# FFN by half tiles: two W1 chunks for 256 tokens to a unit, and the last tile's first two blocks normed at mid-tile

## Chip, cores and metric

The kernel runs on one core of one Trainium2 chip. The metric is device time in microseconds (us) of one execution; the median of several runs counts. TensorE is called PE, VectorE DVE, ScalarE ACT, GpSimd POOL; SP is the queue that issues the transfers.

## The reference

8192 tokens of 512 features pass through two blocks, each with a layer norm ahead and one behind, and a residual. The second block is the one that the change touches; its weights are made ternary (-1, 0, 1).

```python
def _layernorm(x, eps=1e-05):
    m = jnp.mean(x, axis=-1, keepdims=True); v = jnp.var(x, axis=-1, keepdims=True)
    return (x - m) / jnp.sqrt(v + eps)

# attention-like block: projection, gate, depthwise convolution of 3, scan, output projection, norm
uv = x @ in_proj_w + in_proj_b                 # u, v: 512 each
v_local = dwconv(silu(v)); h = a * h + ssm_b * v_local; y = ssm_c * h + ssm_d * v_local
out = layernorm((u * silu(y)) @ out_proj_w + out_proj_b + x) * ln_w + ln_b
# FFN block
h = gelu(x @ ternary(W1).T + b1)               # W1: 2048 x 512
out = h @ ternary(W2).T + b2                   # W2: 512 x 2048
# both
x = x + _layernorm(attn(_layernorm(x)))
x = x + _layernorm(ffn(_layernorm(x)))
```

## The kernel before

The tokens are taken in 16 tiles (NT) of 512 (TT). A tile is four blocks (NB) of 128 tokens, one token to a partition. Matmul operands are split into a high and a low half in f16, so that two or three f16 matmuls stand for one in f32; the ternary weights are exact in fp8 and need no split.

**Steps.** Every engine runs its own hand-written order, and semaphores join them. From step s = 3 on a loop over `LATER` does the same on all engines: step s works on the FFN of tile fa = s - 2, on the gate, output projection and norms of tile c = s - 1, on the first norm and the v projection of tile n = s + 1, and on the final norm and store of tile e = s - 3 (`tiles`, line 257). On ACT and DVE each piece of work carries a number (the `AT_...` constants, lines 54 to 70), and `run` (line 81) issues the pieces in the order of these numbers; the FFN's unit j has numbers near j, so 13.3 means "after unit 13's gelu". PE's order is written out in lines 733 to 769.

**The FFN** (fa) of a tile goes in 16 units (FC = 2048/128), one for each chunk of 128 rows of W1:

- `f1(t, j)` (line 537, PE): 8 matmuls of 512 columns into one of two PSUM banks `f1b`: for each of 4 k, the W1 chunk as weights and the high, then the low half of the transposed tile `x3T` as moving data. Its first unit waits for the transposes of all four blocks (`wait_tile`, line 290), every unit for the gelu of two units before, which frees the bank.
- `gelu(t, j)` (line 1603, ACT): PSUM to `gg`, bias from the chunk's b1. `hi(t, j)` (line 1613, ACT) rounds it to f16, `lo(t, j)` (line 801, DVE) makes the rest.
- `f2(t, j)` (line 567, PE): for each of the four blocks q, two matmuls with a 128 x 128 part of h as weights and the W2 chunk (512 columns) as moving data, added up in four banks `f2b[q]`. It follows f1 by a lag of 4 units (`LAG`), in the last tile by 5 (`LAG_END`). Its first unit waits until the four `f_add` of the tile before have read the banks.

In steps before the last two, f1 of units 0 to 8 comes first, with f2 of 0 to 4 in it (five f1 stand in a row at the start), then u, the rest of these f2, o, half of v, and then f1 of units 9 to 15 (again several in a row) with the other f2 and the rest of v.

**The final norm** of a tile is done one step later: `f_add` (line 811, DVE) reads `f2b[j]`, scales it and adds b2 into `hb`; `f_stats` and `aggr` make mean and variance, POOL's `rstd_f` (line 2063) the factors, ACT's `ffn_norm` (line 1628) applies them, POOL's `finish` (line 2081) adds the residual, SP stores. f_add(0) waits for the last unit of f2 of its tile, and with it all four.

**The last tile** ends block by block: `f2_last` (line 556) does the last five units for block 0, then for block 1, 2 and 3, each block signalled by `f2_sum`. Behind all units DVE runs lines 1589 to 1598: for each block `last_block` (f_add, stats, aggregate), and `last_sum` with the residual; block 3 goes through `last_centre` and `last_out`. `less_shift` (line 979), which subtracts a part of block-wise means from the residual, comes at 13.3 for all four blocks. ACT norms blocks 0 to 2 behind its last unit (lines 2019 to 2021), POOL makes the factors of each block (`rstd_last`, line 2071).

**SP** (lines 455 to 469) issues in each step the four stores of tile e, the load of a later tile, and the transposes t1 and t3. The transposes of `x3T` for the next tile wait for f1's last unit of the present one.

Of the kernel before, what the change touches and what calls it, by code (L numbers as in the profile page):

```python
# [24 lines left out]
P = 128  # L25
D = 512
TT = 512
NB = TT // P
KC = D // P
LAG = 4  # L30
X_SLOTS = 4
G_SLOTS = 5
H_SLOTS = 6
T_SLOTS = 4
EPS = 1e-5
ACT_SCALE = 2048.0
# [7 lines left out]
ACT = mybir.ActivationFunctionType  # L44
# [3 lines left out]
BIN, CW, CB, LA, SB, SC, SD, B1 = 0, 8, 20, 24, 28, 32, 36, 40  # L48
# [15 lines left out]
AT_SILU_LAST, AT_GATE_LAST, AT_GATE_HI_LAST = 16.15, (15.0, 15.1), 16.5  # L64
AT_LO_LAST = (7.65, 8.95, 9.6, 10.6, 11.65, 12.2, 12.9)
AT_T3_HI_PAIR = (16.2, 16.4, 16.6, 16.8)
AT_XC = 13.3
AT_LO_PAIR = (0.45, 1.3, 1.9, 2.4, 3.4, 4.6, 6.0, 7.3)
LAG_END = 5
AT_V = (8.9, 8.95, 16.3, 17.2)  # L70


W1_CHUNK, W2_CHUNK = "w1", "w2"
# [7 lines left out]
def run(items):  # L81

    for _, work in sorted(items, key=lambda item: item[0]):
        work()


def spread(at, step, works):

    return [(at + step * i, w) for i, w in enumerate(works)]


def build(nc, x, w_in, w_out, w1t, w2t, params, rows, out):
# [21 lines left out]
    place = {chunk: o for o, chunk in enumerate(ORDER)}  # L114

    with ExitStack() as ctx:
# [11 lines left out]
        w1 = sb("w1", [P, KC, FF], F8)  # L128
# [153 lines left out]
        def wait_transposed(eng, m):  # L282

            kind, t, j = blocks[m]
            if (kind, t) == ("t3", 0):
                eng.wait_ge(x3_mm, halves_x3.index((1, j)) + 1)
            else:
                eng.wait_ge(transposed[m % T_SLOTS], 16 * by_dma[m])

        def wait_tile(eng, kind, t):  # L290

            for j in range(NB - T_SLOTS, NB):
                wait_transposed(eng, block_no[kind, t, j])

        def bank(kind, t, i):
            if (kind, t) == ("v", 0):
# [25 lines left out]
        def x3T_of(t):  # L322

            return x1T[:, t % 2] if t == NT - 2 else x3T
# [148 lines left out]
        def _(pe):  # L473
# [63 lines left out]
            def f1(t, j):  # L537
                i = FC * t + j
                if t == 0:
                    pe.wait_ge(w_ok, last_of(W1_CHUNK, range(KC * (j // BQ), KC * (j // BQ) + KC)))  # L540
                if i < 2:
                    pe.wait_ge(h_ok, i + 1)
                if j == 0 and t > 0:
                    wait_tile(pe, "t3", t)
                elif j == 0:
                    pe.wait_ge(x3_cp, len(halves_x3))
                if i >= 2:
                    pe.wait_ge(gelu_ok, i - 1)
                b, src = f1b[i % 2], x3T_of(t)
                for k in range(KC):  # L550
                    w = w1[:, k, j * P:(j + 1) * P]
                    pe.matmul(b[:, :], w, src[:, k, :], start=k == 0, stop=False)  # L552
                    mm = pe.matmul(b[:, :], w, src[:, KC + k, :], start=False, stop=k == KC - 1)  # L553
                mm.then_inc(f1_mm, 1)

            def f2_last():

                for q in range(NB):
                    for j in range(FC - LAG_END, FC):
                        if q == 0:  # L560
                            pe.wait_ge(hl_ok, FC * (NT - 1) + j + 1)
                        i, qs = FC * (NT - 1) + j, slice(q * P, (q + 1) * P)
                        pe.matmul(f2b[q][:, :], h_hi[:, i % H_SLOTS, qs], w2[:, j, :], start=False, stop=False)
                        mm = pe.matmul(f2b[q][:, :], h_lo[:, i % H_SLOTS, qs], w2[:, j, :], start=False, stop=j == FC - 1)
                    mm.then_inc(f2_sum, 1)

            def f2(t, j):
                i = FC * t + j
                if j == 0 and t > 0:
                    pe.wait_ge(f_ok, NB * t)  # L570
                elif j == 0:
                    pe.wait_ge(h_ok, NB)
                    pe.wait_ge(v_ok, 3 * KC)
                    pe.wait_ge(thr_ok, 4)
                    pe.wait_ge(u_cp, 2)
                pe.wait_ge(hl_ok, i + 1)
                if t == 0:
                    pe.wait_ge(w_ok, place[W2_CHUNK, j] + 1)
                for q in range(NB):
                    qs = slice(q * P, (q + 1) * P)  # L580
                    pe.matmul(f2b[q][:, :], h_hi[:, i % H_SLOTS, qs], w2[:, j, :], start=j == 0, stop=False)  # L581
                    mm = pe.matmul(f2b[q][:, :], h_lo[:, i % H_SLOTS, qs], w2[:, j, :], start=False, stop=j == FC - 1)  # L582
                mm.then_inc(f2_mm, 1)
# [189 lines left out]
        def _(ve_):  # L773
# [35 lines left out]
                                         op0=ALU.mult, op1=ALU.subtract).then_inc(hl_ok, 1)  # L809

            def f_add(e, j):
                if e == NT - 1:
                    ve_.wait_ge(f2_sum, j + 1)
                elif j == 0:
                    ve_.wait_ge(f2_mm, FC * (e + 1))
                if e + 1 < NT - 1:
                    ve_.wait_ge(x3_lo, NB * (e + 1) + j + 1)
                else:
                    ve_.wait_ge(out_st[j], 16 * e)
                ve_.scalar_tensor_tensor(out=hb[:, j, :], in0=f2b[j][:, :], scalar=f_inv[:, 0:1], in1=b2_row,  # L820
                                         op0=ALU.mult, op1=ALU.add).then_inc(f_ok, 1)
# [157 lines left out]
            def less_shift(j):  # L979

                t = NT - 1
                xsj = xs[:, t % X_SLOTS, j, :]
                ve_.wait_ge(rs_ok[2], NT)
                ve_.tensor_scalar(xsj, xsj, c0[:, t % 4, j:j + 1], None, ALU.subtract).then_inc(xc_ok, 1)

            def last_block(j):

                f_add(NT - 1, j)
                f_stats(NT - 1, j)
                aggr(4, NT - 1, j)  # L990
# [5 lines left out]

            def last_out(j):

                ve_.wait_ge(cen_ok, 1)
                ve_.wait_ge(rs_ok[4], NT + j)  # L1000
                ve_.scalar_tensor_tensor(out=hb[:, j, :], in0=hb[:, j, :], scalar=rs4[:, j:j + 1],
                                         in1=xs[:, (NT - 1) % X_SLOTS, j, :], op0=ALU.mult, op1=ALU.add).then_inc(fin_last, 1)

            def last_sum(j):

                ve_.wait_ge(fn_ok, NB * (NT - 1) + j + 1)
                ve_.tensor_tensor(hb[:, j, :], hb[:, j, :], xs[:, (NT - 1) % X_SLOTS, j, :], ALU.add).then_inc(fin_last, 1)

# [494 lines left out]
            for s in LATER:  # L1503
# [4 lines left out]
                if s == NT:  # L1508
                    items += norms(c) + [(at, lambda j=j: t_lo("t3", c, j)) for j, at in enumerate(AT_T3_LO_LAST)]
                if s == NT + 1:  # L1510
                    items += spread(AT_XC, .01, [lambda j=j: less_shift(j) for j in range(NB)])
                if c is not None and s < NT:
                    items += conv_scan(c)
                if fa is not None:
# [52 lines left out]
                if s == NT - 1:  # L1567
# [18 lines left out]
                        aggr(4, NT - 3, j)  # L1586
                    for j in range(NB):
                        aggr(1, NT - 1, j)
            ve_.wait_ge(xc_ok, NB)
            last_block(0)  # L1590
            last_block(1)
            last_sum(0)
            last_block(2)
            last_sum(1)
            last_block(3)
            last_centre(3)
            last_sum(2)
# [4 lines left out]
        def _(act):  # L1602
            def gelu(t, j):
                i = FC * t + j
                act.wait_ge(f1_mm, i + 1)
                if i < G_SLOTS:
                    act.wait_ge(w_ok, place[W1_CHUNK, i] + 1)
                if i >= G_SLOTS:
                    act.wait_ge(hl_ok, i - G_SLOTS + 1)
                act.activation(gg[:, i % G_SLOTS, :], f1b[i % 2][:, :], ACT.Gelu,  # L1610
                               bias=par[:, B1 + j:B1 + j + 1], scale=1.0 / ACT_SCALE).then_inc(gelu_ok, 1)

# [359 lines left out]
            for s in LATER:  # L1972
# [7 lines left out]
                    items += ffn(fa, range(half(s)))  # L1980
                if s == NT:
                    items += [(at, lambda j=j: t_hi("t3", c, j)) for j, at in enumerate(AT_T3_HI_LAST)]
                run(items)
                if s >= NT:
                    continue
# [30 lines left out]
                if s == NT - 1:  # L2016
                    for b in range(2, KC):
                        gate_hi(NT - 1, b)
            for j in range(NB - 1):
                act.wait_ge(rs_ok[4], NT + j)  # L2020
                ffn_norm(NT - 1, j)


        @block.gpsimd
# [245 lines left out]
```

## Time and profile before

| | |
|---|---|
| runs | 1421.04, 1421.73, 1422.21 us; median 1421.73 |
| span of the profiled execution, first to last instruction | 1420.3 us |
| its own device time | not listed; the runs lie 0.7 to 1.9 us above the span |
| PE busy | 1400.8 us, 6506 matmuls and as many weight loads |
| DVE, ACT, POOL busy | 1116.8, 878.2, 422.3 us |
| mean granted clock of TensorE | 0.999 |

Read it thus: the span is what the profile explains, the median what is measured. A PE record of a 512-column matmul lasts 379 ns, but the next one begins after about 216, since matmuls are pipelined and their ends are modelled. So time on PE is told from starts, not from the sum of the records.

### The profile page before, as it was taken

Reading aid. Unit: us, or ns where it says so; the run is one execution under the profiler, and the core shown is the slowest. Engines: PE = TensorE matmul, PEld = TensorE weight load, DVE = VectorE, ACT = ScalarE, POOL = GpSimd, SP = SyncE. Lnnn points to the kernel's source line nnn. Section 1 sums busy time; section 2 is a strip of 40 time slices with the busy share of each in tenths; the row PEclk is TensorE's granted clock in tenths of the full one; section 3 lists DMA queues with packets and bytes.
Section 4 is the critical chain, followed back from the end, with each engine's and each line's share of the span. In section 5 each row is a group of like instructions: output and inputs, shape, how many; then the busy total and the mean of one; then the engine's idle time right before and its main releaser. Section 6 shows DMA issues by size and latency. Waiting matters only on the chain.

```text
span 1420.3 us, 18989 instructions
## 1 busy us (share of the span) xinstructions
PE 1400.8 (99%) x6506; PEld 640.0 (45%) x6506; DVE 1116.8 (79%) x1889; ACT 878.2 (62%) x1264; POOL 422.3 (30%) x522
## 2 busy tenths in 40 slices
PE   7999999999999999999999999999999999999997
PEld 4444444444444444444444444444444444444443
DVE  7999987868779686796867878677796877998744
ACT  7999665656556565675656756565565656753443
POOL 5234241322314232042331413223142321523221
PEclk9999999999999999999999999999999999999999
DMA  8703221211311122121311203113111221001200
GB/s 245 254 36 90 60 83 20 78 30 38 82 30 60 30 61 59 30 66 25 89 30 31 82 16 82 31 38 82 31 60 30 53 67 30 30 1 30 60 31 30
DMA packets 155984, 82.00 MB, mean 58 GB/s; under 512 B 132720, under 2 KB 132720, under 8 KB 155760
## 3 DMA queue, kind: packets, MB, share of 16 engines
q1 hardware_dynamic: 155888, 80.79, 22.0%
q8 instruction: 51, 0.84, 0.2%
q14 instruction: 45, 0.37, 0.1%
HBM read 31.49 MB, written 16.78 MB: 34 GB/s over the span
## 4 chain that ended last, share of the span: by engine, by line
PE 85%; DVE 4%; issue 3%; POOL 1%; ACT 0%; POOLq 0%; DVEq 0%; ACTq 0%
PE f2b L581 14%; PE f2b L582 14%; PE f1b L552 14%; PE f1b L553 14%; PE misc L520 6%; PE misc L519 6%; PE misc L518 6%; PE misc L533 3%; PE misc L534 3%; PE misc L532 3%; DVE bn L789 1%; DVE vl L865 0%; DVE vl L874 0%; DVE ring L807 0%; POOL rsc L2038 0%
## 5 line engine op out<-in xcount | busy, mean ns | idle before, releaser
L581 PE MATMUL f2b<-w,ring 128*128 128x512 fp8e5 x1004 | 380.5, 379 | 1.2 <-DVE ring L807 0.9
L582 PE MATMUL f2b<-w,ring 128*128 128x512 fp8e5 x1004 | 380.5, 379 | 0.0
L552 PE MATMUL f1b<-x3T,w 128*128 128x512 f16 x960 | 363.8, 379 | 0.1
L553 PE MATMUL f1b<-x3T,w 128*128 128x512 f16 x960 | 363.8, 379 | 0.0
L1610 ACT ACTIVATE ring<-f1b,par 128x512 f32<-128x512 f32 x256 | 175.2, 684 | 227.8 <-PE f1b L553 227.5
L2037 POOL TENSOR_SCALAR ve<-mv 128x4 f32<-128x4 f32 (+2 forms) x89 | 35.4, 398 | 725.5 <-DVE mv L799 725.4
L807 DVE SCALAR_TENSOR_TENSOR ring<-ring,f_sc 128x512 f16<-128x512 f32 x256 | 212.5, 844 | 37.6 <-ACT ring L1620 37.4
L1620 ACT ACTIVATE ring<-ring,f_sc 128x512 f16<-128x512 f32 x256 | 180.1, 710 | 0.0
L518 PE MATMUL misc<-x1T,win_hi 128*128 128x512 f16 x456 | 172.8, 379 | 0.0
L520 PE MATMUL misc<-x1T,win_lo 128*128 128x512 f16 x456 | 172.8, 379 | 0.0
L519 PE MATMUL misc<-x1T,win_hi 128*128 128x512 f16 x456 | 172.8, 379 | 0.0
L581 PEld LDWEIGHTS f2b<-w,ring 128*128 128x128 f16 x1004 | 98.2, 98 | 121.1 <-DVE ring L807 2.4
L582 PEld LDWEIGHTS f2b<-w,ring 128*128 128x128 f16 x1004 | 98.2, 98 | 118.0
L552 PEld LDWEIGHTS f1b<-x3T,w 128*128 128x128 fp8e5 x960 | 93.9, 98 | 114.4 <-issue 1.5
L553 PEld LDWEIGHTS f1b<-x3T,w 128*128 128x128 fp8e5 x960 | 93.9, 98 | 112.7
L1729 ACT ACTIVATE vb<-misc,par,inv_sig 128x512 f32<-128x512 f32 x54 | 41.9, 776 | 140.3 <-PE misc L520 140.1
L789 DVE BATCH_NORM_STATS2 bn<-hb 128x6 f32<-128x512 f32 x184 | 118.8, 679 | 0.2
L865 DVE SCALAR_TENSOR_TENSOR vl<-vb,par,vl 128x512 f32<-128x512 f32 x128 | 105.9, 866 | 0.9 <-POOL vb L2142 0.8
L2093 POOL TENSOR_TENSOR hb<-hb,row 128x512 f32<-128x512 f32 x56 | 80.7, 1444 | 85.7 <-ACT hb L1661 85.7
L2083 POOL TENSOR_TENSOR hb<-hb,xs 128x512 f32<-128x512 f32 x60 | 99.6, 1687 | 18.6 <-ACT hb L1631 18.6
L532 PE MATMUL misc<-wo_hi,g_hi 128*128 128x512 f16 x240 | 91.0, 379 | 0.4 <-DVE g_lo L909 0.3
L533 PE MATMUL misc<-wo_lo,g_hi 128*128 128x512 f16 x240 | 91.0, 379 | 0.0
(227 smaller groups left out, 2015.3 us busy)
## 6 DMA issues: line engine op xcount, KB each, us to landing
out_dram<-hb SPq DMA_DIRECT2D x64, 256.0 KB, 2.0
xs<-x_dram SPq DMA_DIRECT2D x14, 1024.0 KB, 5.4
ring<-w1t_dram SPq DMA_DIRECT2D x3, 1024.0 KB, 13.2
stage<-w2t_dram SPq DMA_DIRECT2D x3, 1024.0 KB, 8.0
x1T<-tp SPq DMA_TRANSPOSE x68, 3.1
xs<-x_dram SPq DMA_DIRECT2D x4, 256.0 KB, 3.4
stage<-w_in_dram SPq DMA_DIRECT2D x4, 256.0 KB, 5.7
xs<-x_dram SPq DMA_DIRECT2D x2, 512.0 KB, 7.2
```

Of the source, the lines that this page charges most:

```text
L518: pe.matmul(o[:, :], wh, x1T[:, s_, k, :], start=k == 0, stop=False)
L519: pe.matmul(o[:, :], wh, x1T[:, s_, KC + k, :], start=False, stop=False)
L520: mm = pe.matmul(o[:, :], wl, x1T[:, s_, k, :], start=False, stop=k == KC - 1)
L532: pe.matmul(out_[:, :], g_hi[:, k, js], wo_hi[:, k, :], start=c > 0 and k == 0, stop=False)
L533: pe.matmul(out_[:, :], g_hi[:, k, js], wo_lo[:, k, :], start=False, stop=False)
L552: pe.matmul(b[:, :], w, src[:, k, :], start=k == 0, stop=False)
L553: mm = pe.matmul(b[:, :], w, src[:, KC + k, :], start=False, stop=k == KC - 1)
L581: pe.matmul(f2b[q][:, :], h_hi[:, i % H_SLOTS, qs], w2[:, j, :], start=j == 0, stop=False)
L582: mm = pe.matmul(f2b[q][:, :], h_lo[:, i % H_SLOTS, qs], w2[:, j, :], start=False, stop=j == FC - 1)
L807: ve_.scalar_tensor_tensor(out=h_lo[:, i % H_SLOTS, :], in0=gg[:, i % G_SLOTS, :], scalar=f_sc[:, 0:1], in1=h_hi[:, i % H_SLOTS, :], op0=A ...
L1610: act.activation(gg[:, i % G_SLOTS, :], f1b[i % 2][:, :], ACT.Gelu, bias=par[:, B1 + j:B1 + j + 1], scale=1.0 / ACT_SCALE).then_inc(gelu_o ...
L1620: act.activation(h_hi[:, i % H_SLOTS, :], gg[:, i % G_SLOTS, :], ACT.Copy, scale=f_sc[:, 0:1]).then_inc(hh_ok, 1)
```

## The change

From tile 1 on, a unit is no longer one W1 chunk for 512 tokens, but the two chunks p and p + 8 for one half (256 tokens) of the tile: units 0 to 7 do blocks 0 and 1, units 8 to 15 blocks 2 and 3. Tile 0 stays as it was.

- f1: 16 matmuls of 256 columns where 8 of 512 were; a bank holds the two chunks side by side. Unit 0 waits for the transposes of blocks 0 and 1 alone, unit 8 for those of blocks 2 and 3.
- gelu: two activations of 256 columns, each with its chunk's bias. hi and lo stay one instruction of 512 each.
- f2: 8 matmuls of 512 columns as before, now 2 blocks x 2 chunks x 2 halves. Unit 0 waits for f_add of the blocks 0 and 1 of the tile before, unit 8 for those of 2 and 3.
- f_add(0) waits for unit 7 of its tile, f_add(2) for unit 15.
- Last tile: f2_last handles blocks 2 and 3 only, with 20 matmuls each (it was four blocks of 10). DVE's last_block(0) and (1) move to 10.3 and 12.3, last_sum(0) and (1) to 14.25 and 15.22, less_shift to 9.45, 10.45, 11.45, 12.45; ACT's norms of blocks 0 and 1 to 13.3 and 14.3. Behind the units stay blocks 2 and 3.

```diff
-AT_XC = 13.3
+AT_XC = 9.45
+AT_FIRST_LAST = (10.3, 12.3)
+AT_FIRST_LAST_NORM, AT_FIRST_LAST_OUT = (13.3, 14.3), (14.25, 15.22)
...
+    PAIRS = FC // 2
+
+    def unit(j):
+
+        h, p = divmod(j, PAIRS)
+        return h, (p, p + PAIRS)
+
+    def half_done(t, h):
+
+        return FC * t + (PAIRS if t > 0 and h == 0 else FC)
...
-                if j == 0 and t > 0:
-                    wait_tile(pe, "t3", t)
+                if j % PAIRS == 0 and t > 0:
+                    wait_blocks(pe, "t3", t, range(2 * (j // PAIRS), 2 * (j // PAIRS) + 2))
...
+                if t > 0:
+                    h, chunks = unit(j)
+                    for n, chunk in enumerate(chunks):
+                        for k in range(KC):
+                            w, o_ = w1[:, k, chunk * P:(chunk + 1) * P], b[:, n * TH:(n + 1) * TH]
+                            pe.matmul(o_, w, src[:, k, h * TH:(h + 1) * TH], start=k == 0, stop=False)
+                            mm = pe.matmul(o_, w, src[:, KC + k, h * TH:(h + 1) * TH], start=False, stop=k == KC - 1)
+                    mm.then_inc(f1_mm, 1)
+                    return
...
-                for q in range(NB):
+                for q in (2, 3):
                     for j in range(FC - LAG_END, FC):
-                        if q == 0:
+                        if q == 2:
                             pe.wait_ge(hl_ok, FC * (NT - 1) + j + 1)
...
+            def f2_block(t, j, q):
+
+                i, (h, chunks) = FC * t + j, unit(j)
+                for n, chunk in enumerate(chunks):
+                    qs = slice(n * TH + (q - 2 * h) * P, n * TH + (q - 2 * h + 1) * P)
+                    pe.matmul(f2b[q][:, :], h_hi[:, i % H_SLOTS, qs], w2[:, chunk, :],
+                              start=chunk == 0, stop=False)
+                    mm = pe.matmul(f2b[q][:, :], h_lo[:, i % H_SLOTS, qs], w2[:, chunk, :],
+                                   start=False, stop=chunk == FC - 1)
+                return mm
...
-                if j == 0 and t > 0:
-                    pe.wait_ge(f_ok, NB * t)
+                if j % PAIRS == 0 and t > 0:
+                    pe.wait_ge(f_ok, NB * (t - 1) + 2 + 2 * (j // PAIRS))
...
-                if e == NT - 1:
-                    ve_.wait_ge(f2_sum, j + 1)
-                elif j == 0:
-                    ve_.wait_ge(f2_mm, FC * (e + 1))
+                if e == NT - 1 and j >= 2:
+                    ve_.wait_ge(f2_sum, j - 1)
+                elif j % 2 == 0:
+                    ve_.wait_ge(f2_mm, half_done(e, j // 2))
...
-                    items += spread(AT_XC, .01, [lambda j=j: less_shift(j) for j in range(NB)])
+                    items += spread(AT_XC, 1, [lambda j=j: less_shift(j) for j in range(NB)])
+                    items += [(at, lambda j=j: last_block(j)) for j, at in enumerate(AT_FIRST_LAST)]
+                    items += [(at, lambda j=j: last_sum(j)) for j, at in enumerate(AT_FIRST_LAST_OUT)]
...
-            ve_.wait_ge(xc_ok, NB)
-            last_block(0)
-            last_block(1)
-            last_sum(0)
             last_block(2)
-            last_sum(1)
             last_block(3)
             last_centre(3)
             last_sum(2)
...
+                if t > 0:
+                    for n, chunk in enumerate(unit(j)[1]):
+                        ts = slice(n * TH, (n + 1) * TH)
+                        ins = act.activation(gg[:, i % G_SLOTS, ts], f1b[i % 2][:, ts], ACT.Gelu,
+                                             bias=par[:, B1 + chunk:B1 + chunk + 1], scale=1.0 / ACT_SCALE)
+                    ins.then_inc(gelu_ok, 1)
+                    return
...
+                if s == NT + 1:
+                    items += [(at, lambda j=j: last_norm(j)) for j, at in enumerate(AT_FIRST_LAST_NORM)]
...
-            for j in range(NB - 1):
-                act.wait_ge(rs_ok[4], NT + j)
-                ffn_norm(NT - 1, j)
+            last_norm(2)
```

## Rows read from the trace of the kernel before

**Rows 1.** The page: busy time by engine, and the chain that ended last.

```profile
PE 1400.8 (99%) x6506; PEld 640.0 (45%) x6506; DVE 1116.8 (79%) x1889; ACT 878.2 (62%) x1264; POOL 422.3 (30%) x522
...
PE f2b L581 14%; PE f2b L582 14%; PE f1b L552 14%; PE f1b L553 14%; PE misc L520 6%; PE misc L519 6%; PE misc L518 6%; PE misc L533 3%; PE misc L534 3%; PE misc L532 3%; DVE bn L789 1%; DVE vl L865 0%; DVE vl L874 0%; DVE ring L807 0%; POOL
```

**Rows 2.** Waits of PE: us in total, times, longest.

```profile
PE f1b L588 <- ACT tp L1704: 7.9, 1, 7.9
...
PE f2b L581 <- DVE ring L807: 0.9, 2, 0.8
```

**Rows 3.** Timeline of PE (start, us), first matmuls of two tiles' f1.

```profile
253.06 0.38 PE L552 MATMUL f1b<-x3T,w 128*128 128x512 f16 x1
...
771.05 0.38 PE L552 MATMUL f1b<-x3T,w 128*128 128x512 f16 x1
```

**Rows 4.** Groups of instructions, f1's first matmuls on PE: busy us, mean ns | idle.

```profile
L552 PE MATMUL f1b<-x3T,w 128*128 128x512 f16 x960 | 363.8, 379 | 0.1
```

**Rows 5.** 128-column matmuls: timeline of PE, and durations (min/median/max) of two lines.

```profile
81.88 0.61 PE L615 MATMUL f1b<-ident_h,tp 128*128 128x128 f16 x8
...
L615 PE MATMUL f1b<-ident_h,tp x16: 219/219/230, 81.9 to 85.6; 128*128 128x128 f16 x16
...
51.69 0.83 PE L605 MATMUL f1b<-ones 128*128 128x128 f32 x6
...
L605 PE MATMUL f1b<-ones x6: 273/275/275, 51.7 to 52.2; 128*128 128x128 f32 x6
```

**Rows 6.** Timeline of PE at two tile boundaries, last of f2 and first of f1.

```profile
857.17 0.38 PE L582 MATMUL f2b<-w,ring 128*128 128x512 fp8e5 x1
857.53 0.38 PE L552 MATMUL f1b<-x3T,w 128*128 128x512 f16 x1
...
1029.98 0.38 PE L582 MATMUL f2b<-w,ring 128*128 128x512 fp8e5 x1
...
1030.45 0.38 PE L552 MATMUL f1b<-x3T,w 128*128 128x512 f16 x1
```

**Rows 7.** ACT: Sign of 512 and of 2048 columns (groups), gelu and hi in the timeline.

```profile
L1758 ACT ACTIVATE w<-ring,thr 128x512 fp8e5<-128x512 f32 x4 | 2.9, 728 | 0.0
...
L1746 ACT ACTIVATE w<-ring,thr 128x2048 fp8e5<-128x2048 f32 x2 | 3.9, 1994 | 0.2 <-DVE thr L1186 0.2
...
515.71 0.69 ACT L1610 ACTIVATE ring<-f1b,par 128x512 f32<-128x512 f32 x1 [1.04 <-PE f1b L553]
516.29 0.71 ACT L1620 ACTIVATE ring<-ring,f_sc 128x512 f16<-128x512 f32 x1
```

**Rows 8.** Timelines of ACT and PE: gelu of unit 9, first matmul of f1(11).

```profile
571.33 0.69 ACT L1610 ACTIVATE ring<-f1b,par 128x512 f32<-128x512 f32 x1
...
572.49 0.38 PE L552 MATMUL f1b<-x3T,w 128*128 128x512 f16 x1
```

**Rows 9.** Timeline of DVE: the four f_add at a boundary.

```profile
512.26 2.73 DVE L820 SCALAR_TENSOR_TENSOR hb<-f2b,f_inv,row 128x512 f32<-128x512 f32 x4 [3.99 <-PE f2b L582]
```

**Rows 10.** Timeline in the last steps: PE behind DVE's lo, DVE behind POOL.

```profile
1273.77 2.08 DVE L963 SCALAR_TENSOR_TENSOR xs<-hb,rsc,xs 128x512 f32<-128x512 f32 x3 [1.52 <-POOL c L2061]
...
1276.57 0.39 PE L581 MATMUL f2b<-w,ring 128*128 128x512 fp8e5 x1 [0.77 <-DVE ring L807]
...
1331.54 0.39 PE L581 MATMUL f2b<-w,ring 128*128 128x512 fp8e5 x1 [0.17 <-DVE ring L807]
```

**Rows 11.** Timelines of PE and DVE at the end: last matmul, f_add(1), last_sum(1), f_add(3).

```profile
1412.49 0.38 PE L564 MATMUL f2b<-w,ring 128*128 128x512 fp8e5 x1
...
1408.59 0.75 DVE L820 SCALAR_TENSOR_TENSOR hb<-f2b,f_inv,row 128x512 f32<-128x512 f32 x1 [0.41 <-PE f2b L564]
...
1412.99 0.66 DVE L1007 TENSOR_TENSOR hb<-hb,xs 128x512 f32<-128x512 f32 x1
1413.57 0.75 DVE L820 SCALAR_TENSOR_TENSOR hb<-f2b,f_inv,row 128x512 f32<-128x512 f32 x1
```

**Rows 12.** Timeline of DVE in the last tile: lo(10).

```profile
1390.06 0.75 DVE L807 SCALAR_TENSOR_TENSOR ring<-ring,f_sc 128x512 f16<-128x512 f32 x1 [2.70 <-ACT ring L1620]
```

More of the change, by code:

```diff
@@ L66 @@
 AT_T3_HI_PAIR = (16.2, 16.4, 16.6, 16.8)
-AT_XC = 13.3
+AT_XC = 9.45
+AT_FIRST_LAST = (10.3, 12.3)
+AT_FIRST_LAST_NORM, AT_FIRST_LAST_OUT = (13.3, 14.3), (14.25, 15.22)
 AT_LO_PAIR = (0.45, 1.3, 1.9, 2.4, 3.4, 4.6, 6.0, 7.3)
 LAG_END = 5
+TH = TT // 2
 AT_V = (8.9, 8.95, 16.3, 17.2)
@@ L288, in wait_transposed, with wait_blocks @@
                 eng.wait_ge(transposed[m % T_SLOTS], 16 * by_dma[m])
+        def wait_blocks(eng, kind, t, js):
+            for j in js:
+                wait_transposed(eng, block_no[kind, t, j])
         def wait_tile(eng, kind, t):
-            for j in range(NB - T_SLOTS, NB):
-                wait_transposed(eng, block_no[kind, t, j])
+            wait_blocks(eng, kind, t, range(NB))
         def bank(kind, t, i):
@@ L556, in f2_last @@
             def f2_last():
-                for q in range(NB):
+                for q in (2, 3):
                     for j in range(FC - LAG_END, FC):
-                        if q == 0:
+                        if q == 2:
                             pe.wait_ge(hl_ok, FC * (NT - 1) + j + 1)
-                        i, qs = FC * (NT - 1) + j, slice(q * P, (q + 1) * P)
-                        pe.matmul(f2b[q][:, :], h_hi[:, i % H_SLOTS, qs], w2[:, j, :], start=False, stop=False)
-                        mm = pe.matmul(f2b[q][:, :], h_lo[:, i % H_SLOTS, qs], w2[:, j, :], start=False, stop=j == FC - 1)
+                        mm = f2_block(NT - 1, j, q)
                     mm.then_inc(f2_sum, 1)
+            def f2_block(t, j, q):
[7 more added lines that the diff above has]
+                return mm
             def f2(t, j):
                 i = FC * t + j
-                if j == 0 and t > 0:
-                    pe.wait_ge(f_ok, NB * t)
+                if j % PAIRS == 0 and t > 0:
+                    pe.wait_ge(f_ok, NB * (t - 1) + 2 + 2 * (j // PAIRS))
                 elif j == 0:
@@ L576, in f2 @@
                 pe.wait_ge(hl_ok, i + 1)
-                if t == 0:
-                    pe.wait_ge(w_ok, place[W2_CHUNK, j] + 1)
+                if t > 0:
+                    for q in range(2 * (j // PAIRS), 2 * (j // PAIRS) + 2):
+                        mm = f2_block(t, j, q)
+                    mm.then_inc(f2_mm, 1)
+                    return
+                pe.wait_ge(w_ok, place[W2_CHUNK, j] + 1)
                 for q in range(NB):
@@ L997, in last_out @@
             def last_out(j):
+                ve_.wait_ge(xc_ok, j + 1)
                 ve_.wait_ge(cen_ok, 1)
@@ L1004, in last_sum @@
             def last_sum(j):
+                ve_.wait_ge(xc_ok, j + 1)
                 ve_.wait_ge(fn_ok, NB * (NT - 1) + j + 1)
@@ L1609, in gelu @@
                     act.wait_ge(hl_ok, i - G_SLOTS + 1)
+                if t > 0:
+                    for n, chunk in enumerate(unit(j)[1]):
[3 more added lines that the diff above has]
+                    ins.then_inc(gelu_ok, 1)
+                    return
                 act.activation(gg[:, i % G_SLOTS, :], f1b[i % 2][:, :], ACT.Gelu,
@@ L1632, in ffn_norm, with last_norm @@
                                scale=rs4[:, j:j + 1]).then_inc(fn_ok, 1)
+            def last_norm(j):
+                act.wait_ge(rs_ok[4], NT + j)
+                ffn_norm(NT - 1, j)
             def centre_tap(c, b):
```

## The prediction

> **What bounds the kernel now.** I read the page first. TensorE (PE) is busy for 1400.8 of the 1420.3 us of the span, and the chain that ended last lies nearly all on it, in the matmuls of the projections and of the two FFN products [rows 1]. So I asked what PE waits for. The list of its waits holds 7.9 us once at the start, and behind that little: the one that concerns the FFN is 0.9 us in two waits [rows 2]. A change can win only four things: columns through PE, time per column, the rare waits, and the stretch after the last matmul. It can lose by making a matmul dearer, or by making PE wait for ScalarE (ACT), VectorE (DVE) or a transfer. A busy share of 99% doesn't say how dense the matmuls are, because a record of 379 ns covers its successor. The starts say it: from the first matmul of tile 2's f1 (253.06) to that of tile 8's (771.05) lie six steady tiles of 400 matmuls (128 each for f1 and f2, 48 each for u, v and o), so 517.99/2400 = 215.8 ns from start to start [rows 3].
>
> **f1 in halves.** In tiles 1 to 15 a unit of f1 issued 8 matmuls of 512 columns and now issues 16 of 256. That is 15 x 16 x 8 = 1920 matmuls (line 552 has 64 records for each of the 15 tiles whose f1 reads x3T, 960 [rows 4], and line 553 as many), which become 3840 with the same columns in all. The price is what a matmul costs beyond its columns. No row has 256 columns. The nearest are the 128-column f16 matmuls of the x3 transposes: eight span 0.61 us, the last of them 0.219 long, so (0.61 - 0.219)/7 = 55.9 ns from start to start [rows 5]. Between 128 and 512 columns that makes (215.8 - 55.9)/384 = 0.4165 ns a column, which is 2.4 GHz, and leaves 55.9 - 53.3 = 2.5 ns that each matmul pays whatever its length. Twice 256 columns is then about 218.4 ns instead of 215.8: 2.6 ns x 1920 = **+5.0 us**, all on PE. Weight loads double too. Every matmul has a load of its own (6506 of each [rows 1]), and the transposes keep 55.9 ns with theirs, so matmuls 109 ns apart hide them. From below the price is 0 (two halves cost a whole). From above I take the f32 matmuls on 128 columns: six span 0.83 us, the last 0.275, so 111 ns apart [rows 5], and 2 x 111 - 215.8 = 6.2 ns or 11.9 us. I take 5.0, because the transposes have the same type of moving data.
>
> The Trainium skill has a rule against this change: "Each matmul has ~60 cycle overhead on TRN2" (TensorEngine Tiling (Array Packing), Instruction Overhead). By it the 1920 added matmuls would cost 25 ns each, an estimate of 48 us. Starts 55.9 ns apart [rows 5] leave no room for such a surcharge on 53.3 ns of columns, so at this length the trace disagrees.
>
> **f2 and the waits of PE.** A unit of f2 issued 8 matmuls for four blocks and now issues 8 for two: same number, same 512 columns, no cost. f1(t,0) waits for two transposed blocks instead of four, f2(t,0) for two added blocks of the tile before. The rest of each wait moves to unit 8, some 20 us on, when all has long been there. In two of the boundaries before f1(t,0) the step between starts was 0.36 and 0.47 us instead of 0.216 [rows 6], 0.14 and 0.26 us lost where f1's waits stand; at the others it was the usual step. I count both as gone: **-0.4 us** (bound: 0, if it wasn't the later blocks).
>
> **Gelu in halves.** Two activations of 256 columns, each with its own bias, replace one of 512 in 240 units. No row has a 256-column gelu. Sign takes 728 ns for 512 columns and 1994 for 2048, so 0.82 ns a column, and a gelu of 0.69 us frees ACT after 0.58 (515.71 to 516.29) [rows 7]. Halved: 0.58 - 0.21 = 0.37 to the second start, plus 0.69 - 0.21 = 0.48, so 0.85 instead of 0.69: **0.16 us later** per unit, and 39 us more of ACT, which is busy 878 of 1420 [rows 1]. Bounds: 0, and 0.58 if a half costs what a whole does. What hides it: where f1 units follow each other without f2, the bank of f1(j) comes free with gelu(j-2). The tightest is f1(11) at 572.49, with gelu(9) over at 571.33 + 0.69 = 572.02, so 0.47 us [rows 8]; 0.16 fits, 0.58 doesn't. Behind gelu(9) on ACT stand gelu(10) and hi(9); a unit then needs 0.74 + 0.6 us of ACT in the 1.75 us that f1 takes, so nothing piles up. At a tile's start two d_conv stand between gelu(3) and gelu(4), but f1(6), which needs gelu(4), comes after two f2 units. Cost: 0.
>
> **DVE.** At each boundary DVE has been idle 4 us when it takes the four f_add in one go of 2.73 us [rows 9]. Blocks 0 and 1 are complete at mid-tile now, so two f_add move into that idle time, and the DVE work behind them, lo(0) to lo(4) with it, comes up to 1.3 us earlier (the scans at most as early as d_conv, which ACT brings 0.16 later). POOL's rstd_f and finish and SP's stores follow the same work and come no later. None of it is on the path: 0.
>
> **The pair of last tiles.** PE is idle 0.77 us before 1276.57 and 0.17 before 1331.54, for DVE's lo [rows 10]; with the 0.16 by which a record outlasts the step between starts, 0.93 and 0.33 us lost. DVE itself had stood in its norms behind POOL (1.52 us before 1273.77) [rows 10]. That chain starts with o, so f1 units that PE does meanwhile don't delay it: 6 in the first case and some 11 in the second, each 8 x 2.6 ns = 0.02 us longer, come out of the waits. **-0.35 us**, bounds 0 and -1.3 (both gone).
>
> **The end.** The last matmul starts at 1412.49 and is over at 1412.87, but f_add(3) starts at 1413.57, behind last_sum(1), which began at 1412.99 [rows 11]. f_add(1) wasn't so blocked: it started at 1408.59, and its block was complete 20 matmuls before block 3, at 1412.87 - 4.32 = 1408.55 [rows 11]. Now blocks 0 and 1 are normed before, and block 2 is complete 4.3 us ahead of block 3, while its f_add, stats and aggregate take some 1.7. So f_add(3) can start at 1412.91: **-0.65 us** (bounds 0 and -1.4, if POOL's chain behind it also runs undisturbed). Behind it stays what was: stats, aggregate, POOL's power, last_out, and the store whose landing ends the kernel. At mid-tile last_block(0) waits on DVE for f2(7), over at about 1393.9, with lo(10) behind it. lo(10) ran at 1390.06 [rows 12] and f2(10) starts 47 matmuls before the last one, at 1402.35; now lo(10) ends at about 1396.7, still 5.6 us ahead. last_norm(0) waits on ACT for POOL until some 1397.3, with gelu(14) behind it, which f1(14) doesn't release before 1399. Cost: 0; were this cover gone, PE would wait about 1 us once.
>
> **Sum.** +5.0 - 0.4 - 0.35 - 0.65 = +3.6 us, give or take 0.7 from the small terms. The span goes from 1420.3 to 1423.9. What lies around it isn't listed for the profiled execution; the median of the runs is 1.43 us above its span, and I keep that: 1421.73 + 3.6 = **1425.3**.
>
> **Rivals.** (A) Half-length matmuls pay 2.5 ns each: 1425.3, chance 0.64. (B) The other side, not slower: the fixed share vanishes at 256 columns. For it: nothing shows that length. Against: it is there at 128 and at 512. Price 0, so -1.4 in all, 1420.3; it decides once the added matmul costs under 0.7 ns (0.12). (C) They behave as the f32 ones, 111 ns apart, because loads or their dispatch bind in runs of 80; for it, the longest run of short f16 ones in the trace is twelve. +11.9 - 1.4, so 1432.2 (0.08). (D) ACT becomes the releaser: half a gelu costs nearly the whole 0.58, f1(11) waits 0.11 us in each of 13 tiles, and the five f1 in a row at a tile's start run at ACT's pace (1.16 + 0.6 against 1.75), some hundredths each: about +2, 1427.3; against it, the slope of [rows 7] (0.08). (E) The early blocks don't do what they are there for, and block 3 still finds DVE busy: the 0.65 stays, 1425.9 (0.07). (F) Tens of ns on each added matmul: 25 x 1920 = 48 us, 1470 (0.01).
>
> **Numbers.** 0.2%, 2.84 us, is about what a measurement of this kernel can tell from no change, so slower means over 1424.6. A lies 0.7 above that, and a quarter of it falls below (the -1.3 bound, a longer gain at the end); with B that makes 0.28 for no change. A gain of 2.84 us needs B, both waits gone and a shorter chain on POOL: 0.03. Slower 0.69. The range takes in A, D, E and part of the way to B and C: 1422.2 to 1429.0.
>
> **What would show it.** On PE 3840 records of 256 columns, starts about 109.2 ns apart, and a steady tile of 86.66 us instead of 86.33. Pairs still 215.8 apart mean B, 222 mean C. No new wait of PE for gelu (line 1610's); one of 0.1 us in each tile means D. A 256-column gelu near 0.48 us. f_add of block 2, not of block 0, first after each boundary. At the end f_add(3) within 0.1 us of the last matmul's end. The forecast is wrong if the steady tile keeps its 86.33 us, or if a wait recurs in every tile.

## The result and the profile after

Changed kernel: median 1425.1 us of 7 runs (1424.7 to 1427.88), before 1421.73 us; the ratio is 1.0029 with a 95% interval of 1.0018 to 1.004. A second set on another occasion gave 1425.42 against 1422.01, ratio 1.0021 (1.0012 to 1.003). So the change makes the kernel 3.4 us slower, 0.2 to 0.3%, as forecast (1425.3, range 1422.2 to 1429.0). Both intervals lie above 1.

The profiled execution of the changed kernel spans 1425.9 us and took 1427.88, the highest of its seven, so it isn't read as a whole but piece by piece. From the page (busy us by engine, the groups of f1 and of gelu):

```profile
PE 1403.4 (98%) x8426; PEld 825.4 (58%) x8426; DVE 1119.8 (79%) x1889; ACT 911.8 (64%) x1504; POOL 414.2 (29%) x522
...
L573 PE MATMUL f1b<-x3T,w 128*128 128x256 f16 x1792 | 397.5, 273 | 0.0
...
L1652 ACT ACTIVATE ring<-f1b,par 128x256 f32<-128x256 f32 x480 | 201.2, 471 | 227.0 <-PE f1b L574 226.7
```

PE has 8426 matmuls, 1920 more than in [rows 1]; ACT has 240 instructions and 33.6 us more (39 forecast). The waits of PE (us in total, times, longest):

```profile
PE f1b L628 <- ACT tp L1755: 7.8, 1, 7.8
PE misc L550 <- DVE hb L968: 2.2, 1, 2.2
PE f1b L628 <- DMA x1T<-tp: 2.0, 3, 1.5
...
PE f2b L597 <- DVE ring L847: 0.8, 1, 0.8
```

There is no wait for a gelu. The second line is a single stall in the straight-line start of the kernel, which the change doesn't touch. It is why the first f1 of tile 1 starts at 168.99 instead of 166.73. The second profiled execution of the same kernel had it at 166.43 and a span of 1422.8.

Timeline of PE, first matmul of f1 in tiles 2 and 8, and four of the starts in a row:

```profile
255.64 0.27 PE L573 MATMUL f1b<-x3T,w 128*128 128x256 f16 x1
255.75 0.27 PE L574 MATMUL f1b<-x3T,w 128*128 128x256 f16 x1
255.86 0.27 PE L573 MATMUL f1b<-x3T,w 128*128 128x256 f16 x1
255.97 0.27 PE L574 MATMUL f1b<-x3T,w 128*128 128x256 f16 x1
...
775.56 0.27 PE L573 MATMUL f1b<-x3T,w 128*128 128x256 f16 x1
```

Six steady tiles take 519.92 us instead of 517.99 [rows 3]: 86.65 us a tile instead of 86.33, 0.32 more for 128 more matmuls, which is 2.5 ns each. The starts, taken over the 3469 steps from one 256-column matmul of f1 on x3T straight to the next, are 109.17 ns apart.

Timeline of DVE at the same boundary as in [rows 9], and in the last microseconds, with PE's last matmul and POOL's last two (L2089 raises the variance to a power; the texts below call it POOL's power):

```profile
515.80 1.41 DVE L860 SCALAR_TENSOR_TENSOR hb<-f2b,f_inv,row 128x512 f32<-128x512 f32 x2 [2.81 <-PE f2b L599]
...
1418.86 0.38 PE L599 MATMUL f2b<-w,ring 128*128 128x512 fp8e5 x1
...
1419.27 0.75 DVE L860 SCALAR_TENSOR_TENSOR hb<-f2b,f_inv,row 128x512 f32<-128x512 f32 x1 [2.62 <-PE f2b L599]
...
1421.41 0.68 DVE L1049 TENSOR_TENSOR hb<-hb,xs 128x512 f32<-128x512 f32 x1
1422.64 0.75 DVE L1042 SCALAR_TENSOR_TENSOR hb<-hb,rs,xs 128x512 f32<-128x512 f32 x1 [0.55 <-POOL rs L2089]
...
1421.05 0.51 POOL L2088 TENSOR_SCALAR ve<-mv 128x1 f32<-128x1 f32 x1 [2.86 <-DVE mv L839]
1421.64 0.86 POOL L2089 TENSOR_TENSOR rs<-ve,mhalf 128x1 f32<-128x1 f32 x1
```

DVE takes two f_add at the boundary, not four. At the end it is idle for 2.6 us before f_add(3), which starts 0.03 us after the last matmul is over (1418.86 + 0.38) instead of 0.70 [rows 11].

The kernel before and both profiled executions of the changed one, cut at the first f1 of a tile (us; the last column runs to the last instruction):

| | tile 1 to 13 | 13 to 14 | 14 to 15 | 15 to last matmul's end | behind it |
|---|---|---|---|---|---|
| before | 1036.39 | 98.74 | 55.60 | 55.42 | 7.46 |
| change | 1039.84 | 99.10 | 55.57 | 55.74 | 6.68 |
| change, second execution | 1039.84 | 99.11 | 55.57 | 55.74 | 6.13 |
| difference, first execution | +3.45 | +0.36 | -0.03 | +0.32 | -0.78 |

The differences of the first execution add up to +3.32 us, against 3.4 in the medians. The last column counts from the modelled end of the last matmul, as the texts below do; from its start it would be 0.38 more (7.83 and 7.05, the numbers in one of the expectations).

### The profile page after: what moved, and what is told of

The parts are those of the page before. It is cut to its first block, busy times and chain, and to the rows that moved or that the text cites. A ratio compares the mean times of both kernels' runs of the same rounds, so it can differ in the third digit from the quotient of the medians.

```text
span 1425.9 us, 23101 instructions
## 1 busy us (share of the span) xinstructions
PE 1403.4 (98%) x8426; PEld 825.4 (58%) x8426; DVE 1119.8 (79%) x1889; ACT 911.8 (64%) x1504; POOL 414.2 (29%) x522
## 4 chain that ended last, share of the span: by engine, by line
PE 86%; DVE 4%; issue 2%; DMA 0%; ACT 0%; POOL 0%; POOLq 0%; DVEq 0%; ACTq 0%
PE f1b L573 14%; PE f1b L574 14%; PE f2b L597 14%; PE f2b L599 14%; PE misc L538 6%; PE misc L536 6%; PE misc L537 6%; PE misc L550 3%; PE misc L552 3%; PE misc L551 3%; PE f2b L622 1%; PE f2b L621 1%; DVE w L1234 0%; DVE g_lo L949 0%; DMA xs<-x_dram 0%
## 5 line engine op out<-in xcount | busy, mean ns | idle before, releaser
L573 PE MATMUL f1b<-x3T,w 128*128 128x256 f16 x1792 | 397.5, 273 | 0.0
L574 PE MATMUL f1b<-x3T,w 128*128 128x256 f16 x1792 | 397.5, 273 | 0.0
L597 PE MATMUL f2b<-w,ring 128*128 128x512 fp8e5 x960 | 363.9, 379 | 0.8 <-DVE ring L847 0.8
L599 PE MATMUL f2b<-w,ring 128*128 128x512 fp8e5 x960 | 363.8, 379 | 0.0
L1652 ACT ACTIVATE ring<-f1b,par 128x256 f32<-128x256 f32 x480 | 201.2, 471 | 227.0 <-PE f1b L574 226.7
L847 DVE SCALAR_TENSOR_TENSOR ring<-ring,f_sc 128x512 f16<-128x512 f32 x256 | 200.4, 796 | 30.1 <-ACT ring L1666 30.0
L574 PEld LDWEIGHTS f1b<-x3T,w 128*128 128x128 fp8e5 x1792 | 175.4, 98 | 32.6
L573 PEld LDWEIGHTS f1b<-x3T,w 128*128 128x128 fp8e5 x1792 | 175.3, 98 | 32.5
L597 PEld LDWEIGHTS f2b<-w,ring 128*128 128x128 f16 x960 | 93.9, 98 | 101.4 <-DVE ring L847 1.8
L599 PEld LDWEIGHTS f2b<-w,ring 128*128 128x128 f16 x960 | 93.9, 98 | 99.5
L905 DVE SCALAR_TENSOR_TENSOR vl<-vb,par,vl 128x512 f32<-128x512 f32 x128 | 119.2, 970 | 0.9 <-POOL vb L2193 0.8
## 6 DMA issues: line engine op xcount, KB each, us to landing
ring<-w1t_dram SPq DMA_DIRECT2D x3, 1024.0 KB, 13.5
```

Source lines behind the costliest of these rows:

```text
L573: pe.matmul(o_, w, src[:, k, h * TH:(h + 1) * TH], start=k == 0, stop=False)
L574: mm = pe.matmul(o_, w, src[:, KC + k, h * TH:(h + 1) * TH], start=False, stop=k == KC - 1)
L597: pe.matmul(f2b[q][:, :], h_hi[:, i % H_SLOTS, qs], w2[:, chunk, :], start=chunk == 0, stop=False)
L847: ve_.scalar_tensor_tensor(out=h_lo[:, i % H_SLOTS, :], in0=gg[:, i % G_SLOTS, :], scalar=f_sc[:, 0:1], in1=h_hi[:, i % H_SLOTS, :], op0=A ...
L1652: ins = act.activation(gg[:, i % G_SLOTS, ts], f1b[i % 2][:, ts], ACT.Gelu, bias=par[:, B1 + chunk:B1 + chunk + 1], scale=1.0 / ACT_SCALE)
```

## Experiments

The kernel before was run again beside the experiments: its median was 1422.76 us (26 runs) beside e1, e2, e3 and e6, and 1422.01 us (31 runs) beside e4, e5, e7 and a2. Each ratio below is against these.

### f1 alone in halves (e1_f1_256)

```diff
+                if t > 0:
+                    for n in range(TT // 256):
+                        cs = slice(n * 256, (n + 1) * 256)
+                        for k in range(KC):
+                            w = w1[:, k, j * P:(j + 1) * P]
+                            pe.matmul(b[:, cs], w, src[:, k, cs], start=k == 0, stop=False)
+                            mm = pe.matmul(b[:, cs], w, src[:, KC + k, cs], start=False, stop=k == KC - 1)
+                    mm.then_inc(f1_mm, 1)
+                    return
```

> The kernel before with nothing but f1's matmuls of tiles 1 to 15 cut into two of 256 columns (same chunk, same unit, same gelu, same waits). Theory (each matmul pays 2.5 ns beyond its columns): starts of f1 109.2 ns apart, steady tile 86.65 us instead of 86.33, in all +4.8 us less about 0.2 that the waits of the last tiles swallow; no gain at the end: 1426.3 if before is at 1421.7. Rival (the steady tile grew because of the half-tile order, the second gelu or the waits at unit 8): starts still 107.9 ns apart, tile 86.33, no change against before.

Measured: 1427.16 us, ratio 1.0033 (1.0023 to 1.0044), 4.4 us slower than before. Steady tile 86.65 us, starts 109.17 ns apart. Between two tiles:

```profile
252.99 0.27 PE L555 MATMUL f1b<-x3T,w 128*128 128x256 f16 x1
253.10 0.27 PE L556 MATMUL f1b<-x3T,w 128*128 128x256 f16 x1
```

The whole growth of the steady tile comes with the cut of the matmuls alone. The end stayed at 7.46 us. From tile 13 to 14 it took 98.94 us, 0.20 more than before: of the 0.32 for its matmuls, 0.12 came out of PE's wait for lo.

### f1 in quarters (e2_f1_128)

The same edit with 128 in place of 256.

> The kernel before with f1's matmuls of tiles 1 to 15 cut into four of 128 columns, runs of up to 160 short matmuls. Theory (2.5 ns a matmul): 128 x 3 x 2.5 = 0.96 us more a tile, 87.29 us, starts 55.9 ns apart, in all +14.4 us. Rival (in long runs weight loads or the supply of instructions bind, as twelve short ones in a row could not show): starts clearly over 56 ns, new idle time of PE's loads put down to issue, more than 1 us a tile; at 81 ns apart it would be 128 x 4 x 25 ns = 12.8 us a tile.

Measured: 1434.74 us (4 runs), ratio 1.0088 (1.0069 to 1.0107), 12.0 us slower. Groups of f1's matmuls and of their weight loads:

```profile
L556 PE MATMUL f1b<-x3T,w 128*128 128x128 f16 x3584 | 412.6, 219 | 0.0
...
L555 PEld LDWEIGHTS f1b<-x3T,w 128*128 128x128 fp8e5 x3584 | 350.6, 98 | 13.9 <-issue 0.4
```

The steady tile took 87.29 us, 0.96 more than before, and the starts were 55.8 ns apart over 7053 steps. The loads waited 0.4 us in all for issue. So runs of 160 short matmuls keep the price of 2.5 ns each; in them neither loads nor the supply of instructions bind. The median is 2.4 us under the 14.4 of the theory. In the profiled execution the stretches from tile 1 to the last matmul grew by 13.5 us (the stalls at boundaries and for lo gave way for the rest), and its end was 0.6 us shorter than in before's, with POOL's power at 0.60 us instead of 1.02; the remaining 0.9 us lies within the spread of the medians.

### Gelu alone in halves (e3_gelu_halves)

```diff
+                if t > 0:
+                    for ts in (slice(0, TT // 2), slice(TT // 2, TT)):
+                        ins = act.activation(gg[:, i % G_SLOTS, ts], f1b[i % 2][:, ts], ACT.Gelu,
+                                             bias=par[:, B1 + j:B1 + j + 1], scale=1.0 / ACT_SCALE)
+                    ins.then_inc(gelu_ok, 1)
+                    return
```

> The kernel before with nothing but the gelu of tiles 1 to 15 cut into two activations of 256 columns. Theory (0.16 us later per unit, hidden behind 0.47 us and more): no change, within 0.5 us; steady tile 86.33 us, gelu records of 471 ns. Rival (ACT's lateness reaches PE): waits of PE for the gelu line in each tile, some tenths of a us each, +2 us or more in all.

Measured: 1422.88 us, ratio 0.9994 (0.9985 to 1.0003): no change, and no wait of PE for gelu. But there is one place where the lateness gets through. Timelines of ACT and DVE in tile 13:

```profile
1258.65 0.84 ACT L1612 ACTIVATE ring<-f1b,par 128x256 f32<-128x256 f32 x2 [0.89 <-PE f1b L553]
1259.38 0.72 ACT L1626 ACTIVATE ring<-ring,f_sc 128x512 f16<-128x512 f32 x1
...
1260.13 0.75 DVE L807 SCALAR_TENSOR_TENSOR ring<-ring,f_sc 128x512 f16<-128x512 f32 x1 [0.28 <-ACT ring L1626]
```

DVE waits 0.28 us for hi(13,9), where it waited 0.15 before, with the norms queued behind it. From there to PE's wait for lo, DVE's work comes 0.15 us late against the tile's start, the step between starts at that wait is 1.30 us instead of 1.15, and tile 13 to 14 took 98.89 us, 0.15 more than before, with not one matmul more. But it comes back: PE arrives late at its next wait for lo too, but that lo comes when it did before (128.4 us after the tile's start in both), the step there is 0.40 us instead of 0.55, and tile 14 to 15 took 55.45 us, 0.15 less. From tile 13 to 15 both kernels take 154.3 us, within 0.01 of each other.

### The last tile alone by half tiles (e6_last_tile_only)

The change with its conditions `t > 0` made `t == NT - 1` in f1, f2, gelu and half_done; tiles 1 to 14 keep the old units and waits.

> Half-tile units in the last tile alone, tiles 1 to 14 as before; last tile's first two blocks normed at mid-tile as in the change. Theory: 128 more matmuls cost 0.3 us, the end after the last matmul shrinks from 7.83 us to 7.05 (0.78), steady tile 86.33: 0.45 us faster than before, about 1421.3, and 3.8 us faster than the change. Rival (the shorter end needs the half tiles throughout, or was chance): the end stays at 7.8 us, 1422.0.

Measured: 1421.81 us, ratio 0.9997 (0.9988 to 1.0007). Steady tile 86.333, last tile 0.32 us longer, 6.67 us behind the last matmul. The end is shorter without half tiles elsewhere, and the loss of the change is gone. Against before it can't be told from no change, so the 0.45 us faster of the theory is neither shown nor excluded.

### Norms of the last tile behind all units (e4_norms_behind)

```diff
-                    items += [(at, lambda j=j: last_block(j)) for j, at in enumerate(AT_FIRST_LAST)]
-                    items += [(at, lambda j=j: last_sum(j)) for j, at in enumerate(AT_FIRST_LAST_OUT)]
...
+            last_block(0)
+            last_block(1)
+            last_sum(0)
             last_block(2)
+            last_sum(1)
             last_block(3)
```

ACT's norms of blocks 0 and 1 stand behind its last unit as well.

> The changed kernel, but the last tile's blocks 0 and 1 are added, normed and summed behind all units, as before, instead of at mid-tile; order of f1 and f2 as in the change. Theory 1 (the end is shorter because block 3 is complete 20 matmuls behind block 2, which leaves DVE time to clear what came earlier): DVE works blocks 0 to 2 off from lo(15) on, some 6 us, and is free when block 3 is complete: f_add(3) still within 0.3 us of the last matmul's end, time as the change within 0.3 us. Rival (the norms at mid-tile are what shortens the end): f_add(3) starts 0.7 us or more behind the last matmul's end, 0.7 us slower than the change.

Measured: 1425.44 us, ratio 1.0026 (1.0017 to 1.0036); the change beside it had 1425.42. Timeline of DVE:

```profile
1412.37 0.74 DVE L860 SCALAR_TENSOR_TENSOR hb<-f2b,f_inv,row 128x512 f32<-128x512 f32 x1
...
1417.33 0.74 DVE L860 SCALAR_TENSOR_TENSOR hb<-f2b,f_inv,row 128x512 f32<-128x512 f32 x1
...
1419.92 0.75 DVE L860 SCALAR_TENSOR_TENSOR hb<-f2b,f_inv,row 128x512 f32<-128x512 f32 x1 [0.32 <-PE f2b L599]
```

DVE starts on block 0 at 1412.37 and still has 0.32 us in hand when block 3 is complete; 6.68 us follow the last matmul, as in the change. So what shortens the end is the order of the blocks in f2, not the norms at mid-tile. The expectation's reason, that block 3 is complete 20 matmuls behind block 2 instead of 10, is only a part of it. Blocks 0 and 1 are complete since mid-tile, so DVE starts on block 0 7.5 us before the last matmul's end; in the kernel before it started 6.4 us before it, and waited 0.41 us more for block 1 [rows 11]. There block 0 was complete 30 matmuls before the end, at about 1406.4, and DVE had been idle for 1.20 us. Timeline of DVE, the kernel before:

```profile
1406.49 0.75 DVE L820 SCALAR_TENSOR_TENSOR hb<-f2b,f_inv,row 128x512 f32<-128x512 f32 x1 [1.20 <-issue]
```

And with the norms behind, block 2's f_add, at 1417.33, started some 1.7 us after its block was complete. What each part is worth alone was not tried.

### The old waits at tile boundaries (e5_full_waits)

```diff
-                if j % PAIRS == 0 and t > 0:
-                    wait_blocks(pe, "t3", t, range(2 * (j // PAIRS), 2 * (j // PAIRS) + 2))
+                if j == 0 and t > 0:
+                    wait_tile(pe, "t3", t)
...
-                if j % PAIRS == 0 and t > 0:
-                    pe.wait_ge(f_ok, NB * (t - 1) + 2 + 2 * (j // PAIRS))
+                if j == 0 and t > 0:
+                    pe.wait_ge(f_ok, NB * t)
```

and f_add(0) waits for the whole tile, but in the last.

> The changed kernel with the old waits at tile boundaries: f1(t,0) for all four transposed blocks, f2(t,0) for all four f_add, f_add(0) for the whole tile. Theory (the late fourth transpose cost PE some tenths at a few boundaries): one to three boundaries with 0.1 to 0.5 us between the last f2 and the first f1, 0.3 to 0.8 us in all, tiles 1 to 13 1040.1 to 1040.6 us instead of 1039.84; f2(t,4) again close behind its lo. Rival (those stalls in the kernel before had another cause, and the change took them away by the shift of its tiles against the transfers): no boundary stalls, 1039.84.

Measured: 1425.71 us, ratio 1.0025 (1.0015 to 1.0034), too near to the change for the medians to part them. In the timeline of PE one boundary stall is back, 0.47 us between starts where 0.22 is usual:

```profile
1032.39 0.38 PE L599 MATMUL f2b<-w,ring 128*128 128x512 fp8e5 x1
1032.86 0.27 PE L573 MATMUL f1b<-x3T,w 128*128 128x256 f16 x1
```

Tile 1 to 13 took 1040.09 us, 0.25 more than in both executions of the change and just under the 1040.1 to 1040.6 of the theory. It is a boundary that stalled before, the second of [rows 6], and also in e1 (0.51 between starts), e2 (0.34), e3, e6 and e7; in no boundary from tile 2 on of the three executions with the new waits (change, its repetition, e4) is there a stall.

The traces also show what PE waits for there. In e3 one boundary, at 512.16, stalls long enough for the list of PE's waits to name it:

```profile
PE f1b L552 <- DMA x3T<-tp: 0.3, 1, 0.3
```

From tile 2 to 13 the seven profiled executions with the old waits have 12 such boundaries, and in each of them the last of the four transposes of x3T had landed only 0.24 to 0.25 us before f1 began; in the two of the kernel before, 0.25. In the changed kernel f1 began before it had landed: by 0.66 us in tile 1, 0.30 in tile 5 and 0.08 in tile 11, and in the repetition by 0.46 and 0.18 in the last two. There the old wait would have held PE up.

### Block 2 earlier (e7_block2_early)

e6, with block 3's part of unit 10 put off into f2_last, and last_sum(2) ahead of last_block(3).

> Half-tile units in the last tile alone, and block 2 complete 24 matmuls ahead of block 3 instead of 20 (block 3's part of unit 10 is put off), so that last_sum(2) runs before f_add(3) and no longer beside POOL's power. Theory (DVE and POOL slow each other: POOL's power took 1.02 us beside two DVE instructions, 0.57 alone): POOL's power at the end 0.6 us instead of 0.86, the end after the last matmul 6.3 to 6.45 us instead of 6.67, 0.7 us faster than before in all. Rival (POOL's duration there is chance, or the centring alone slows it): power stays at 0.86 or more and the end at 6.6.

Measured: 1421.45 us, ratio 0.9996 (0.9987 to 1.0005). Timeline of DVE and POOL at the end:

```profile
1412.67 0.69 DVE L1054 TENSOR_TENSOR hb<-hb,xs 128x512 f32<-128x512 f32 x1 [2.49 <-ACT hb L1682]
...
1415.45 0.21 POOL L2093 TENSOR_SCALAR ve<-mv 128x1 f32<-128x1 f32 x1 [3.72 <-DVE mv L844]
1415.74 0.60 POOL L2094 TENSOR_TENSOR rs<-ve,mhalf 128x1 f32<-128x1 f32 x1
```

The power took 0.60 us and the end 6.13, shorter than the theory's 6.3 to 6.45. Against before the medians can't tell it from no change. Nor does the short end prove the theory, as the next run shows.

### The change once more (a2_change_again)

> The changed kernel itself once more, on the same chip as the other three. Theory (its profiled execution had a stall of 2.4 us near 123 us by chance): first f1 of tile 1 at 166.0 to 166.5 us instead of 168.99, tiles 86.65 us, end 6.68 us after the last matmul, span near 1423.1. Rival (the stall comes with the change): again at 168.9 or later.

Measured: 1425.42 us, first f1 of tile 1 at 166.43, tile 86.65, span 1422.8. The stall at the start isn't the change's. POOL's last two beside DVE's:

```profile
1418.92 0.67 DVE L1049 TENSOR_TENSOR hb<-hb,xs 128x512 f32<-128x512 f32 x1
...
1418.51 0.21 POOL L2088 TENSOR_SCALAR ve<-mv 128x1 f32<-128x1 f32 x1 [2.86 <-DVE mv L839]
1418.80 0.60 POOL L2089 TENSOR_TENSOR rs<-ve,mhalf 128x1 f32<-128x1 f32 x1
```

Here last_sum(2) ran beside the power, and it still took 0.60; the end was 6.13 us. So an end of 6.13 us doesn't need e7's edit, and the rival "chance" stands.

## Why the prediction was right, step by step

**f1, +5.0.** Right, and 0.2 too high: 2.5 ns x 1920 = 4.8 us, from 0.32 us in each of 15 tiles. e1 shows it with the cut alone, e2 at three times the dose (0.96 us a tile). The line through 128 and 512 columns held at 256: 109.2 ns forecast, 109.17 measured. Rivals B (0), C (111 ns apart) and F (25 ns on each) fall with that number. One step of the count was right by luck: the 960 records that the prediction names are those of tiles 0 to 13 and 15. Tile 0 isn't changed, and tile 14, which is, reads its operand from x1T (64 records more on each line). Both make 15 tiles. The Trainium skill's rule of some 60 cycles a matmul (TensorEngine Tiling (Array Packing), Instruction Overhead), read as a cost added to each one, doesn't hold at 128 and more columns: the trace has 2.5 ns, or 6 cycles at 2.4 GHz. The same section gives a matmul with a free dimension of 1 the latency of one with 60, which is a floor for short ones; no run here is that short.

**Boundaries, -0.4.** Right: twelve tiles grew by 12 x 0.32 = 3.84 us and came out 3.45 longer, and e5 brought a part of it back. The late fourth transpose is what PE waited for, as the landings above show. In the other executions with the old waits the boundaries of these twelve tiles cost 0.1 to 0.9 us.

**Gelu, 0.** A half took 471 ns (0.47 forecast), both 0.84, and D falls: no PE wait for a gelu. The 0 is right in the sum, but with some luck. I had looked at who waits for gelu on PE, not at DVE's lo(13,9), which follows its hi by 0.03 us and has the norms of the last but one tile queued behind it. That way 0.15 us reached PE, and only because a second wait stood behind the first did it come back (e3: +0.15 and -0.15).

**The pair of last tiles, -0.35.** Right in the sum, not in its places. Without the gelu, e1 did what was forecast: of its 0.64 us the first wait took 0.12 (0.13 counted) and the second 0.18 (0.22 counted), so tile 13 to 15 took 0.34 more. The change took 0.33 more, otherwise divided. The late lo(13,9) gives +0.36 up to tile 14, with 1.21 us between starts at the first wait instead of 1.15, and the wait that stood before 1331.54 [rows 10] is gone whole, 0.33. The first wait in the change:

```profile
1281.45 0.38 PE L599 MATMUL f2b<-w,ring 128*128 128x512 fp8e5 x1
1282.66 0.39 PE L597 MATMUL f2b<-w,ring 128*128 128x512 fp8e5 x1 [0.82 <-DVE ring L847]
```

**The end, -0.65.** f_add(3) came 0.67 us earlier, as forecast; 0.78 in all. The step "behind it stays what was" failed by the rest. POOL's last two instructions come in two states: with the new order they take 0.51 and 0.86 us or 0.21 and 0.60, and the end 6.67 to 6.68 or 6.13 to 6.15 us; with the old order 0.51 and 1.02 or 0.21 and 0.60, and the end 7.46 or 6.88 to 6.89 (e2, e3). So the gain is 0.78 within the first and 0.73 to 0.76 within the second. In the first state the power itself became shorter, 0.86 instead of 1.02. In the second last_out stands behind last_sum(2): with the old order that one waited for ACT's norm of block 2 and began 2.98 us after the last matmul's end (e3), with the new one 2.23 (a2), since that norm was over 0.2 us before the last matmul. Rival E falls. But the reason was given too widely: e4 shows that the norms at mid-tile add nothing to the order of blocks in f2.

The cover at mid-tile held: last_block(0) started at 1400.22, lo(10) ended at 1402.95 and f2(10) began at 1408.71, 5.8 us later (5.6 forecast).

The sum was +3.6, measured +3.32 by stretches and +3.4 by medians. 0.2 was too much for f1 and 0.13 too little for the gain at the end; both errors push the sum the same way, up. The boundaries came out within 0.01 and gelu and the last pair of tiles together within 0.04. The spread within the kernels, some 3 us, is as large as the effect; only many runs and the stretches of the trace part them.

## What to carry to other kernels

Where PE is dense, as here, halving the moving size cost a small fixed price per added matmul, and it could be read beforehand from two other lengths in the same trace: 2.5 ns, in 1920 places 4.8 us for nothing. An end that is better by reordering blocks needs that order in the last tile alone (e6); paid for in fifteen tiles, it is lost. When an engine is made later, look for the instruction on every other engine that follows it by hundredths of a microsecond, and for what is queued behind that one. Then follow the lateness to the next wait of the engine that counts: it may be swallowed there.

## What was not expected

The start of the kernel, which no version here changes, ends at one of two times: first f1 of tile 1 at 166.1 to 167.0 us in eight profiled executions, at 168.99 and 169.62 in two (the change, e4). In the late ones DVE's instructions last longer. Timeline of DVE, the change and then its repetition:

```profile
112.84 0.69 DVE L829 BATCH_NORM_STATS2 bn<-xs 128x6 f32<-128x512 f32 x1 [0.68 <-DMA xs<-x_dram]
...
116.09 3.75 DVE L949 SCALAR_TENSOR_TENSOR g_lo<-yb,g_sc,g_hi 128x512 f16<-128x512 f32 x4
119.76 3.09 DVE L1234 SCALAR_TENSOR_TENSOR w<-stage,thr,w 128x512 fp8e5<-128x512 f32 x3
```

```profile
115.48 2.73 DVE L949 SCALAR_TENSOR_TENSOR g_lo<-yb,g_sc,g_hi 128x512 f16<-128x512 f32 x4
118.13 2.07 DVE L1234 SCALAR_TENSOR_TENSOR w<-stage,thr,w 128x512 fp8e5<-128x512 f32 x3
```

Four instructions take 3.75 us instead of 2.73 and three 3.09 instead of 2.07, after DVE has waited 0.68 us for a transfer (in e4 0.40 us, and then the same 3.75 and 3.09). The runs show the same step: e6's spans are 1419.4 to 1420.2 seven times and 1422.4 to 1423.4 four times. That a late transfer shifts DVE against POOL's additions, which then slow it, is a guess; it wasn't tried, and the cause stays open. So does what decides between the two durations of POOL's last instructions. They come with either order: of the ten profiled executions five have 0.21 and 0.60 us (e2, e3, e5, e7, a2) and five 0.51 and 0.86 or 1.02 (before, the change, e1, e4, e6). DVE's centring, which begins 0.04 to 0.05 us before POOL's first, lasts 0.54 us in all of the former and 0.48 to 0.49 in all of the latter.
